# Perceiver block, router logits: gate as the weights, token rows in blocks of 32 over the four column quarters

## The reference, cut to what matters

```
xf = layernorm(x).reshape(-1, 1024)
router_logits = xf @ gate_w.T                    # gate_w: (8, 1024)
routing  = softmax(router_logits, axis=1)        # 8 experts
in_scale = routing @ in_channel_scale
out_scale = routing @ out_channel_scale
out = xf * in_scale @ sign(weight).T * out_scale + bias
x = x + out
```

## Time and profile before

| what | us |
|---|---|
| runs shown: median (lowest, highest) of 3 | 435.2 (434.12, 436.86) |
| the profiled execution's own time | 435.73 |
| its span | 433.9 |
| outside the span | 1.83 |
| TensorE busy in it | 372.0 (86%) |
| VectorE, ScalarE, GpSimd busy | 308.2, 260.7, 134.3 |

### The profile page before, as it was taken

One profiled execution on the slowest core, in us unless ns is written; L12 is line 12 of the kernel. 1 busy time (PEld: TensorE's weight loads), 2 busy tenths in 40 slices (PEclk: granted clock), 3 DMA queues, 4 the chain that ended last, 5 costly groups with the idle time before them and its releaser, 6 DMA issues.

```text
span 433.9 us, 9130 instructions
## 1 busy us (share of the span) xinstructions
PE 372.0 (86%) x3712; PEld 247.8 (57%) x3712; DVE 308.2 (71%) x587; ACT 260.7 (60%) x309; POOL 134.3 (31%) x148
## 2 busy tenths in 40 slices
PE   0434954799887989999999999999999999999687
PEld 0113932685442586559755975597559755964254
DVE  7667689998366539767985898589858975594441
ACT  4766896647766767866676568656865731333030
POOL 5210034615121302612261226122712261035031
PEclk9985895799889999999999999999999999999958
DMA  8999997488858875875667576757674001000011
GB/s 316 394 400 409 408 407 287 122 275 355 328 203 266 298 243 173 295 277 163 249 230 263 161 253 236 264 154 260 241 256 134 2 2 50 2 2 2 0 49 50
DMA packets 30384, 91.96 MB, mean 212 GB/s; under 512 B 8256, under 2 KB 8512, under 8 KB 30336
## 3 DMA queue, kind: packets, MB, share of 16 engines
q1 hardware_dynamic: 28464, 84.45, 54.6%
q10 hardware_dynamic: 1872, 6.82, 4.2%
HBM read 85.50 MB, written 4.19 MB: 207 GB/s over the span
## 4 chain that ended last, share of the span: by engine, by line
PE 72%; DVE 10%; ACT 6%; DMA 5%; issue 3%; POOL 2%; SPq 0%; ACTq 0%; DVEq 0%
PE R L1566 10%; PE T L1394 7%; PE R L1346 6%; PE R L1348 6%; PE R L1347 6%; PE R L1430 5%; PE C L1375 5%; DMA ring<-ctx 5%; PE R L1432 5%; PE R L1433 5%; PE T L1517 4%; PE T L1475 3%; ACT b L579 2%; PE R L1459 2%; PE R L1593 1%
## 5 line engine op out<-in xcount | busy, mean ns | idle before, releaser
L579 ACT ACTIVATE b<-ring,quant,qpar 128x2048 uint8<-128x2048 f32 x64 | 132.4, 2093 | 14.8 <-DMA ring<-ctx 8.0
L1430 PE MATMUL R<-T_hi,Wqkv_hi 128*128 128x128 f16 x448 | 80.0, 223 | 0.0
L1432 PE MATMUL R<-T_lo,Wqkv_hi 128*128 128x128 f16 x448 | 79.9, 222 | 0.0
L1433 PE MATMUL R<-T_hi,Wqkv_lo 128*128 128x128 f16 x448 | 79.8, 222 | 0.0
L1375 PE MATMUL C<-b,aT 128*64 128x512 f16 x256 | 38.1, 433 | 16.0 <-ACT b L579 14.1
L330 POOL TENSOR_TENSOR Pr<-Pr,mx 128x512 f32<-128x512 f32 x20 | 20.7, 1044 | 86.5 <-DVE mx L1041 86.5
L1430 PEld LDWEIGHTS R<-T_hi,Wqkv_hi 128*128 128x128 f16 x448 | 45.1, 101 | 1.6
L480 POOL TENSOR_TENSOR Pr<-Pr,mx 128x512 f32<-128x512 f32 x32 | 35.6, 1121 | 33.9 <-DVE mx L1047 33.9
L1432 PEld LDWEIGHTS R<-T_lo,Wqkv_hi 128*128 128x128 f16 x448 | 44.6, 100 | 0.2
L1433 PEld LDWEIGHTS R<-T_hi,Wqkv_lo 128*128 128x128 f16 x448 | 44.6, 100 | 0.0
L1346 PE MATMUL R<-Wo,attT_hi 128*128 128x512 f16 x112 | 43.4, 387 | 0.6 <-DVE attT_lo L1059 0.5
(11 more groups left out here) (167 smaller groups left out, 864.7 us busy)
## 6 DMA issues: line engine op xcount, KB each, us to landing
ring<-ctx SPq DMA_DIRECT2D x64, 1024.0 KB, 6.2
ring<-L_attn_Wo SPq DMA_DIRECT2D x4, 1024.0 KB, 7.5
ring<-L_ffn_weight SPq DMA_DIRECT2D x4, 1024.0 KB, 5.0
Wo<-L_attn_Wqkv SPq DMA_DIRECT2D x7, 544.0 KB, 15.3
X<-x ACTq DMA_DIRECT2D x7, 512.0 KB, 3.4
out<-X ACTq DMA_DIRECT2D x6, 512.0 KB, 6.2
sgn<-L_attn_Wqkv SPq DMA_DIRECT2D x1, 544.0 KB, 18.6
X<-x SPq DMA_DIRECT2D x1, 512.0 KB, 12.6
```

The costliest lines, as they stand in the source:

```text
L579: e.activation(b8[:, c % BRING, :], ring[:, slot, :], ACT.Identity, scale=qR2, bias=qZ2).then_inc(s_rf[slot], 1)
L1430: e.matmul(dst, hi, rows[0], start=k == 0 and g == 0, stop=False, skip_group_check=True)
L1432: e.matmul(dst, hi, rows[1], start=False, stop=False, skip_group_check=True)
L1433: last = e.matmul(dst, lo, rows[0], start=False, stop=k == KT - 1, skip_group_check=True)
```

## The change

The gate becomes the stationary operand, padded with zeros from 8 to 32 columns, and the transposed rows become the moving one, in four blocks of 32 rows. Block j writes its logits to the PSUM partitions 32j to 32j+31, so the four blocks of a chunk go through four different column quarters of the array. In PSUM each 32x32 block then holds experts down and rows across; VectorE's copy out of PSUM becomes a 32x32 transpose of the four blocks into a tile `rl` of 128 x 32, whose first eight columns are the logits as before. The host's table grows from 4 + 64 to 4 + 256 float32 on each partition.

```diff
+BLOCK = 32
...
-        small_sb = sb("small_sb", [P, 4 + KT * E], F32)
-        gate_sb = small_sb[:, 4:].rearrange("p (k e) -> p k e", e=E)
+        small_sb = sb("small_sb", [P, 4 + KT * BLOCK], F32)
+        gate_sb = small_sb[:, 4:].rearrange("p (k e) -> p k e", e=BLOCK)
...
+        rl = sb("rl", [P, BLOCK], F32)
...
-                e.activation(rt[:, E:2 * E], rt[:, 0:E], ACT.Exp, bias=rs[:, 0:1]).then_inc(s_rexp, 1)
+                e.activation(rt[:, E:2 * E], rl[:, 0:E], ACT.Exp, bias=rs[:, 0:1]).then_inc(s_rexp, 1)
...
-                e.tensor_copy(rt[:, 0:E], T[:, bank, 0:E]).then_inc(s_free[bank], 1)
+                e.transpose(rl[:, :], T[:, bank, 0:BLOCK]).then_inc(s_free[bank], 1)
                 e.wait_ge(s_free[bank], s.turn("rl") + 1)
-                e.tensor_reduce(rs[:, 0:1], rt[:, 0:E], AX.X, ALU.max, negate=True).then_inc(s_nmx, 1)
+                e.tensor_reduce(rs[:, 0:1], rl[:, 0:E], AX.X, ALU.max, negate=True).then_inc(s_nmx, 1)
...
-                    last = e.matmul(T[:, bank, 0:E], ln2T[:, k, :], gate_sb[:, k, :],
-                                    start=k == 0, stop=k == KT - 1)
+                    for j in range(P // BLOCK):
+                        at = slice(j * BLOCK, (j + 1) * BLOCK)
+                        last = e.matmul(T[at, bank, 0:BLOCK], gate_sb[:, k, :], ln2T[:, k, at],
+                                        start=k == 0, stop=k == KT - 1)
...
-    t = np.zeros((P, 4 + KT * E), np.float32)
+    t = np.zeros((P, 4 + KT * BLOCK), np.float32)
...
-    t[:, 4:] = gate_w.T.reshape(KT, P, E).transpose(1, 0, 2).reshape(P, KT * E)
+    gate = np.zeros((P, KT, BLOCK), np.float32)
+    gate[:, :, :E] = gate_w.T.reshape(KT, P, E).transpose(1, 0, 2)
+    t[:, 4:] = gate.reshape(P, KT * BLOCK)
```

## The result

The changed kernel takes 428.75 us (median of four runs, 426.47 to 429.75) against 434.66 us (four runs, 433.97 to 436.86) for the kernel before: a ratio of 0.986, 95% interval 0.983 to 0.990. So 6.1 us are gone from the span, where the prediction had 4.45.

What follows compares the result with a forecast made beforehand. TensorE was taken to bound the stages from 154 us on. Seven routers -3.5, tail -1.2 and table +0.25 sum to -4.45 us: 431.3 against the profiled 435.73, median 430.8 us, 8-in-10 range 429.0 to 438.0.

Steps and rivals of the forecast that it cites:

- What bounds the kernel: Stages from 154 us on: TensorE busy 42.95 of 43.02 us, so each nanosecond off its queue is one off the kernel.
- The router's 64 passes: Burst router: 32 products at 0.033 us, 1.06 us, with shape changes 1.26 against 1.76, 0.50 us less per router.
- The lowest bound: Burst router if loads hide wholly: 32 x 0.029 = 0.93, with shape changes 1.13 us, 0.63 saved.
- The step from one quarter to the next: Between products in the router: nearly free, 0.003 us, resting on two halves; named most likely to be wrong.
- Quarters in turn: Rival 1, routers: one pass at a time, 1.8 to 2.25 us each, kernel 434.6 to 439.2 us; chance 0.34.
- No overlap: Rival 2, routers: each pass waits for its own load, +2.1 us per burst router, kernel 454 us; chance 0.07.
- The third rival: Bursts: TensorE's passes shrink but another chain keeps stages at 43.0, only the tail gains, 434.2 us; chance 0.05.
- The shape changes: Around each router: 0.15 us in, 0.16 out where 0.056 is usual, 0.20 us added for both.
- The tail: Last router at 1.2 GHz: 2.3 us against 3.57, less 0.1 for VectorE's transpose, net 1.2 us less.
- VectorE: Copy turned transpose: 0.19 to 0.3 us, covered in the bursts, taken as 0.1 us more in the tail.
- The table: Start: 98 KB more ahead of two context pieces in the queue, 0.25 us more.
- No new wait in the bursts: Bursts: nearer waits stay harmless, no new one ends last, so 7 x 0.50 = 3.5 us passes through.

Runs made afterwards that it cites:

- one-quarter kernel: The changed kernel with all 16 passes of one column quarter done before the next quarter's: 436.17 us, ratio 1.003 to the kernel before.
- second timing: The changed kernel run again with no edit, timed together with the kernel before: 426.22 us (six runs), ratio 0.982.

## Why the prediction was right or wrong

**What bounds the kernel: right.** In the stages each nanosecond out of TensorE's queue was a nanosecond of the kernel until TensorE had to wait for something new. Stages without such a wait are 0.90 to 0.94 us shorter, for 0.97 us per router.

**The router's 64 passes: the step that failed.** The prediction said: "the two passes of one product use the same quarter one after the other, then the next quarter follows", and from that 0.033 us for a product and 1.06 for 32. The pace of one quarter was right: 0.030 predicted, 0.0317 measured, and in the one-quarter kernel it is the pace of the whole. What failed is the strict order. A quarter's waiting passes don't hold up those of the other quarters, so four passes go per 0.0317 us, not two passes per 0.033. For a whole burst router, both changes of shape counted, it gave 0.79 us instead of 1.26. The term of the sum was mis-sized: 0.97 us less per router, not 0.50. The lowest bound, "if the load hides wholly and only the stream counts", 1.13 us, had the same fault: with 32 x 0.029 it still let only two passes go per 0.029 us. This is why the measured median, 428.75 us and 426.2 in the second timing, lies under the range, whose lower end was 429.0. The earlier trace rows could have warned: the two halves' matmuls there start at the same time, so two streams of 256 columns were running side by side, and the prediction used the pair's overlap but not what it means for two passes with short streams in four parts. The step from one quarter to the next, which the prediction named as most likely to be wrong, was indeed where it was wrong, on the side that nobody had priced.

**Rivals.** Quarters in turn (1.8 to 2.25 us per router) is what the one-quarter order gives, 1.84, and not what the change has. No overlap, 3.9, is not seen anywhere. The third rival, another chain as long, didn't come about: VectorE's 34.3 and ScalarE's 29.1 us of a stage still lie inside the 42.1.

The Trainium skill (TensorE: Matmul & The Clock Gate, Part 3) lets loads overlap matmuls only over different row groups. Here all loads use all rows, and the 64 pairs of load and matmul start within 0.567 us: this kernel's rows speak against it, as the earlier trace rows did. The floor of about 25 ns from start to start (the same page of the Trainium skill, Back-to-back issue gap) would by an estimate, 64 times 0.025, make at least 1.6 us of 64 passes; the trace has 0.0083 to 0.009 us a pass. By the measurement that floor does not hold between column parts. For passes in one and the same quarter the trace has 0.0317 us, above it.

**The shape changes: near.** 0.15 us in as predicted (0.149), and 0.13 out instead of 0.16 (0.128 from start to start); over two usual steps of 0.056 that is 0.17 together, where 0.20 was taken.

**The tail: right in kind, too small.** Predicted 2.3 us for the router's piece, measured 1.48 including 0.3 of a wait that the prediction didn't see; with `t2` it is 1.64 less instead of 1.2 (2.5 less where `t2` still had the full clock). It looked in the bursts for waits that the shorter router might uncover, and not in the tail, where there was one: ScalarE's second half of `ln2T`.

**VectorE: right.** The transpose takes 0.206 us, inside 0.19 to 0.3. In the bursts it is covered, as this timeline of VectorE in the kernel after shows, against the earlier trace rows:

```profile
202.51 0.69 DVE L891 SCALAR_TENSOR_TENSOR qT_lo<-R,qT_hi 128x512 f16<-128x512 f32 x1 [0.16 <-ACT qT_hi L565]
203.12 0.21 DVE L1098 STREAM_TRANSPOSE rl<-T 128x32 f32<-128x32 f32 x1
...
204.76 0.18 DVE L1112 TENSOR_TENSOR rstack<-rt,rstack 128x16 f16<-128x16 f32 x1
```

The idle time ahead of the read is gone, and the chain ends at 204.94, 1.2 us before its result is used at 206.15. The scores start 0.06 us behind the end of `q_lo` (203.26 against 203.20), so that slack was 0.5 in the prediction and is used up: with a router that is shorter still the scores would wait.

**The table: not resolved.** Its landing took 10.0 us for 130.0 KB against 9.5 for 34.0; the predicted 0.25 us of delay is under the scatter of the start.

**No new wait in the bursts: wrong in part.** No engine's result is late, but TensorE itself has two idle times, 0.22 and 0.68 us in the profile after. The prediction had asked how fast 128 instructions can come in 1.06 us, but only within one router and not for what the delivery might lack some microseconds later. Both end 1.4 to 1.5 us after an instruction packet, so what it left out is the wait for instructions.

Open are: what makes an instruction packet come late, and why a router of 128 passes brings so many waits; whether the gains of tail and bursts add up; whether the quarter of the array or its PSUM partitions set the 0.0317 us; and the price of the table.

## What to carry to other kernels

When a product with few output columns is put on the column quarters, alternate the quarters from pass to pass: the same 64 passes took 0.69 us over four, 1.05 over two and 1.84 in turn, and only the overlap pays, not the smaller weights. In a stage that TensorE bounds, read the pace from starts and not from durations, look for the copy that the longer product used to cover, and look for idle time without a releaser once there are many small matmuls. Where there is some, see whether a packet of the instruction queue ends shortly before each idle time does, by the same distance each time: then TensorE waited for its instructions. A few empty instructions at the head can move such a wait but did not reliably remove it. Count what it costs from start to start.

## What the runs showed of the hardware

- Passes of different column quarters with all 128 rows run side by side, loads too: four passes in 0.0317 us at full clock and in 0.0533 at half. Within one quarter (and its 32 PSUM partitions) it is one pass (float32, 32 columns loaded, 32 moved) in 0.0317 us.
- A pass seems to start ahead of earlier ones that wait for their own quarter, by three places or so (64 passes in turn took 1.716 us instead of 2.00; the records don't name the quarter).
- A long run of such passes goes at 0.0083 us for a load and a matmul together (128 passes in 1.10 us).
- Changes of shape cost 0.15 us from 128 to 32 columns and 0.13 back from start to start, and 0.25 from 32 columns straight to 64 rows.
- TensorE can wait for its own instructions: 24 idle times of 0.1 to 1.2 us without a releaser all end 1.26 to 1.58 us after the end of a 16 KB packet (256 instructions) on the instruction queue.
